# Graph kernel on one core: building the adjacency blocks with shorter loop bodies on TensorE and VectorE, and W stored from three pair buffers

## The chip, the cores and the metric

One core of a Trainium2 chip runs the whole program. The metric is the device time of one execution in microseconds, lower is better. Times in the profile are counted from the start of the span.

## The reference, cut to what matters

The reference is a chain of four graph layers over N = 3125 nodes (96 features) and E = 103,125 edges sorted by target. Each layer normalizes `x`, applies a graph operator and adds the result to `x`:

```python
h = relu(layernorm(x)); x = x + propagate_10_steps(h)        # counts of edges, degree-scaled
h = relu(layernorm(x)); x = x + gated_edges(h, edge_attr)    # per-edge gates, summed by target
h = relu(layernorm(x)); x = x + two_gcn_layers(h)            # segment_sum(h[src], dst)
h = relu(layernorm(x)); x = x + two_weighted_gcn(h, edge_weight)   # segment_sum(w * h[src], dst)
```

Every `segment_sum(h[src], dst)` is a product with a matrix that depends on the edges alone. The kernel builds two such matrices once, at its start: C, which counts the edges from each source to each target, and W, which sums their weights. This case is about that building stage alone.

## The kernel before

**The stages.** `edge_ranges` makes tables of the edges (to about 50 us), `build_matrices` makes C and W (about 50 to 545 us), `propagate` follows (to about 1137 us), then `gated_edges` (to about 2190 us), and the two GCN stages end the program.

**How the building is tiled.** The 3125 target nodes are padded to NT = 25 node tiles of 128. A node tile has WPT = 16 windows of WIN = 8 nodes, and GW = 4 windows make a group, so there are 400 windows and NG = 100 groups. For a group VectorE makes one-hot operands in one of two buffers: `S` (`sources` on L492, then `weighted` twice on L504, with the weight in two fp16 parts) and `M` (`targets` on L498). GpSimd makes the small columns that `targets` reads (L415, L421), and the column tile `sw` comes in by a DMA for each group (L444). For each window TensorE multiplies three edge tiles in three parts, which is 9 matmuls of 200 columns into one PSUM bank (`products`, L573). Where the table's flag `past` is over 0, there is a fourth edge tile and each of the four windows has 12 matmuls. Code for still more edges (`past > 1`: `one_more` on VectorE, `more_products` on TensorE) is in the loops, but is not executed on these inputs. ScalarE takes each window out of PSUM in two copies, L641 (counts, into the C block) and L645 (weights, into `Wwin`), and SyncE stores W window by window (L459) and C once for a node tile (L461). For `propagate` the C block of the tile before is also transposed, 25 transposes a tile after the second window of each group (`turn`, L592), and copied to `CT` (L632).

**The loops.** VectorE's loop (`four`, L546) has four groups in its body, 25 rounds. Each group's body holds `one_more` four times, once for each window. TensorE does the first node tile in straight code, and its loop (`four`, L619) then has four node tiles in its body, 6 rounds, so that it goes back to its start five times. ScalarE's and SyncE's loops have two node tiles each.

**What orders the work.** Semaphores alone. VectorE may start group g when TensorE has finished group g - 2 (`dve.wait_ge(s_built, g * GW + GW)`, on a counter that starts at 8). TensorE starts group g when VectorE has finished it (`s_made`), and a window when ScalarE has taken out the window four before it (`s_evac`). ScalarE may write a buffer of `Wwin` when the store of the window four before it has landed (`s_wst`); SyncE's queue serves its `sw` loads and its stores in the order of the code.

Of the kernel before, what the change touches and what calls it, by code (L numbers as in the profile page):

```python
# [13 lines left out]
ALU = mybir.AluOpType  # L14
# [19 lines left out]
FRONT = 2 * (GW - 1)  # L34
SWB = 4
SE = 6
NS = 135
# [286 lines left out]

def build_matrices(nc, tab_d, pair_d, key, smod, weight, CT, indeg, spare, C_d, W_d):

# [5 lines left out]
    with ExitStack() as ctx:  # L332
        m = Scope(nc, ctx, "build")
        tab = m.sb("tab", [1, NG + 1, GW + 2], I16)
        colsM = m.sb("colsM", [P, HALF, 2], F16)
# [18 lines left out]
        Sx = m.sb("Sx", [P, PARTS, P], F16)  # L354
        rowh = Cblk[0][:, 0, :]
        win = m.ps("win", [P, 4, 512])
# [16 lines left out]
        s_cst = [m.sem(f"C_stored{b}") for b in range(2)]  # L373
        s_wst = [m.sem(f"W_stored{r}") for r in range(4)]
        block = ctx.enter_context(nc.Block())

        def group_range(eng, regs, g):

            eng.load(regs, tab[0:1, bass.ds(g, 1), :])
            why = "edge_ranges clamps the tables"  # L380
            first = nc.s_assert_within(eng.snap(regs[0]), 0, FRONT + TCLAMP, skip_runtime_bounds_check_because=why)
            ends = [nc.s_assert_within(eng.snap(regs[1 + i]), 1, FRONT + TCLAMP + 1,
                                       skip_runtime_bounds_check_because=why) for i in range(GW)]
            return first, ends

        def group_over(eng, reg, g):
# [5 lines left out]
        def _(pool):  # L392
# [35 lines left out]
            with pool.Fori(0, NG // 2) as pair:  # L428
                columns(0, pair * 2)
                columns(1, pair * 2 + 1)  # L430
            columns(0, NG)

        @block.sync
        def _(sp):
            sp.dma_start(tab[:, :, :], tab_d[0:NG + 1, :].rearrange("(o q) b -> o q b", o=1)).then_inc(s_tab, 16)

            reg = sp.alloc_register("sp_bound")

            def columns(b, g):

                sp.load([reg], tab[0:1, bass.ds(g, 1), 0:1])
                t = nc.s_assert_within(sp.snap(reg), 0, FRONT + TCLAMP,
                                       skip_runtime_bounds_check_because="edge_ranges clamps the tables")
                sp.dma_start(sw[:, b, :, :, :].rearrange("p a t z -> p a (t z)"),  # L444
                             pair_d[:, :, bass.ds(t * 2, 2 * GT)]).then_inc(s_sw[b], 16)

            def store(j, b):

                for u in range(WPT):
                    if u % GW == 0:  # L450
                        g = j * (WPT // GW) + u // GW
# [9 lines left out]
                sp.dma_start(C_d[bass.ds(j, 1), :, :].rearrange("o p c -> p (o c)"),  # L461
                             Cblk[b].rearrange("p k d -> p (k d)")).then_inc(s_cst[b], 16)
# [10 lines left out]
            for r in range(4):  # L473
                sp.wait_ge(s_wst[r], 16 * (NW // 4) + 1)

        @block.vector
        def _(dve):
# [4 lines left out]
            dve.wait_ge(s_tab, 16)  # L482
            regs = [dve.alloc_register(f"dve_bound{r}") for r in range(GW + 2)]
            over = dve.alloc_register("dve_over")
# [10 lines left out]
            def targets(b):  # L495

                shape = [P, CH * GW, HALF, 2]
                nc.vector.tensor_tensor(M[:, b, :, :, :, :].rearrange("p c i a z -> p (c i) a z"),  # L498
                                        colsM[:, :, :].unsqueeze(1).to_broadcast(shape),
                                        kw[:, b, :, :, :].rearrange("p c i z -> p (c i) z").unsqueeze(2).to_broadcast(shape),  # L500
                                        ALU.is_equal)
# [5 lines left out]
            def one_more(b, i, t):  # L507

                dve.wait_ge(s_xused, dve.snap(more) + 1)
                n = dve.snap(more) * 6  # L510
                dve.reg_add(more, more, 1)
                nc.vector.tensor_tensor(kx[:, :], key[:, bass.ds(t, 1)], bases[:, b, i:i + 1], ALU.subtract).then_inc(s_xstep, 1)
                nc.vector.tensor_copy(wx[:, 0:1], weight[:, bass.ds(t, 1)]).then_inc(s_xstep, 1)
# [12 lines left out]
            def group(b, r, g, turn):  # L526
# [24 lines left out]
        def _(pe):  # L551
# [6 lines left out]
            for b in range(2):  # L558
                pe.sem_inc(s_cst[b], 1)
            for r in range(4):  # L560
                pe.sem_inc(s_wst[r], 1)
# [7 lines left out]
            def products(b, i, tiles):  # L569
                for u in tiles:  # L570
                    for part in range(PARTS):
                        out = win[:, i, 0:WC] if part == 0 else win[:, i, WC:2 * WC]
                        mm = pe.matmul(out, S[:, b, part, 2 * i + u, :, :].rearrange("p a z -> p (a z)"),  # L573
                                       M[:, b, u, i, :, :].rearrange("p a z -> p (a z)"),
                                       start=(u == 0 and part == 0), stop=(u == FEW - 1 and part in (0, PARTS - 1)),
# [9 lines left out]
            def turn(j, b, g):  # L585
# [9 lines left out]
            def node_tile(j, b, before):  # L595

                for q in range(WPT // GW):
# [3 lines left out]
                    for i in range(GW):  # L601
# [12 lines left out]
                        products(q % 2, i, range(FEW - 1, FEW)).then_inc(s_built, 1)  # L614
                        if before and i == 1:
                            turn(j - 1, 1 - b, q)
# [9 lines left out]
        def _(act):  # L626
# [9 lines left out]
            def node_tile(j, b, before):  # L636

                act.wait_ge(s_cst[b], (j - b) * 8 + 1)
                for u in range(WPT):
                    act.wait_ge(s_built, j * WPT + u + 1 + 2 * GW)  # L640
                    nc.scalar.activation(Cblk[b][:, :, u * WIN:(u + 1) * WIN],  # L641
                                         win[:, u % 4, 0:WC].rearrange("p (d k) -> p k d", d=WIN),
                                         ACT.Copy, scale=0.5).then_inc(s_evac, 1)
# [1579 lines left out]
def gnn(nc, x, src_cols, dst_cols, dst_rows, attr, w_cols, We, be, Wn, bn, W1, b1, W2, b2,  # L2223
# [10 lines left out]
    with ExitStack() as outer:  # L2234
# [5 lines left out]
        with ExitStack() as inner:  # L2240
# [3 lines left out]
            with ExitStack() as ctx:  # L2244
# [4 lines left out]
                edge_ranges(nc, src_cols, dst_cols, dst_rows, w_cols, tab_d, tabs_d, base_d, row_d, pair_d, key, smod, weight, unscale, CT)  # L2249
                build_matrices(nc, tab_d, pair_d, key, smod, weight, CT, indeg, xs, C_d, W_d)  # L2250
            propagate(nc, x, xs, CT, indeg, src_cols, We, be, Wn, bn, ident, first, P_d, Q_d)
# [45 lines left out]
```

## Time and profile before

| | us |
|---|---|
| median of three runs | 2706.46 |
| lowest and highest of them | 2706.18, 2714.7 |
| the profiled execution, its own time | 2699.71 |
| its span, first to last instruction | 2697.9 |
| building stage in it | about 50 to 545 |

The profiled execution gives durations and waits; its time is 6.75 us below the median of the three runs. A row that groups instructions has their count, their busy time, the mean of one, and the idle time of the engine just before them with what ended it. `PEld` is TensorE's weight load, and an engine name with a `q` is its sequencer (branches and register work).

### The profile page before, as it was taken

What the parts mean: (1) busy time and instruction counts of PE and PEld (TensorE: products, weight loads), DVE (VectorE), ACT (ScalarE), POOL (GpSimd) and SP (SyncE); (2) the same over time, 40 slices, a digit from 0 to 9 for tenths busy, and PEclk for the clock granted to TensorE, in tenths of its full rate; (3) what the DMA queues carried; (4) which work ended last, traced back from release to release, by engine and by line L of the source; (5) the groups of instructions that cost most, each with busy time, mean ns of one, the idle gap of its engine ahead of it and who ended that gap; (6) DMA issues with size and microseconds to landing.
All of it is one profiled execution on the core that took longest, in us unless ns stands there. A gap on an engine that the chain in (4) does not pass through costs nothing. (4 is left out here: it accounts for less than half of the span.)

```text
span 2697.9 us, 55857 instructions
## 1 busy us (share of the span) xinstructions
PE 2221.2 (82%) x18268; PEld 2088.8 (77%) x18269; DVE 1638.3 (61%) x3181; ACT 1356.5 (50%) x2800; POOL 1111.1 (41%) x1225
## 2 busy tenths in 40 slices
PE   2878788869999999687778877788788748779998
PEld 1877777869999999487677777777777648779998
DVE  7888778855433334566565666666666664465465
ACT  1666556643333332165555555555555523257686
POOL 2655556500000000277777777777777702200000
PEclk6999999989999999765555555555555569979999
DMA  1444444410000000444444444444444452096281
GB/s 58 143 131 128 133 128 141 135 45 2 2 2 1 2 2 16 118 118 116 108 113 113 109 117 108 111 115 109 117 109 110 109 213 104 2 385 226 79 292 39
DMA packets 184980, 283.92 MB, mean 105 GB/s; under 512 B 76675, under 2 KB 152678, under 8 KB 179270
## 3 DMA queue, kind: packets, MB, share of 16 engines
q1 hardware_dynamic: 145958, 200.50, 23.4%
q0 software_dynamic: 38688, 79.28, 11.5%
q8 instruction: 171, 2.80, 0.5%
q14 instruction: 163, 1.34, 0.2%
HBM read 210.52 MB, written 69.15 MB: 104 GB/s over the span
## 5 line engine op out<-in xcount | busy, mean ns | idle before, releaser
L1238 POOL DMA_INDIRECT layer_R<-source_terms,layer_srcs x800 | 781.7, 977 | 243.7 <-issue 243.7
L1470 PE MATMUL layer_zp<-layer_right,layer_left 96*128 96x192 f32 x1342 | 471.3, 536 | 178.9 <-DVE layer_left L1257 174.8
L1470 PEld LDWEIGHTS layer_zp<-layer_right,layer_left 96*128 96x128 f32 x1342 | 404.1, 327 | 195.7 <-DVE layer_left L1257 186.7
L1004 PEld LDWEIGHTS layer_acc<-layer_U,graph_CT 128*128 128x128 f16 x6250 | 524.7, 97 | 30.6 <-ACT layer_U L933 21.1
L1004 PE MATMUL layer_acc<-layer_U,graph_CT 128*128 128x192 f16 (+1 forms) x6250 | 529.8, 246 | 22.0 <-ACT layer_U L933 20.0
L573 PE MATMUL build_win<-build_M,build_S 128*128 128x200 f16 x3948 | 382.6, 253 | 127.3 <-DVE build_S L504 77.0
L573 PEld LDWEIGHTS build_win<-build_M,build_S 128*128 128x128 f16 x3948 | 335.3, 99 | 156.9 <-issue 45.6
L1491 PEld LDWEIGHTS layer_acc<-layer_hot,layer_G 128*98 128x98 f32 x1648 | 252.3, 256 | 114.9 <-DVE layer_aggT L1311 114.8
L1491 PE MATMUL layer_acc<-layer_hot,layer_G 128*98 128x32 f32 x1648 | 268.3, 329 | 54.0 <-DVE layer_aggT L1311 53.8
L2209 PE MATMUL layer_acc<-layer_V,layer_turn 128*128 128x96 f32 x2500 | 287.9, 278 | 0.6 <-issue 0.6
L2209 PEld LDWEIGHTS layer_acc<-layer_V,layer_turn 128*128 128x128 f32 x2500 | 286.0, 195 | 0.9 <-issue 0.9
L1416 ACT ACTIVATE layer_y<-layer_R 128x1152 f32<-128x1152 f32 x135 | 156.3, 1158 | 237.3 <-DVE layer_R L1285 237.3
L1285 DVE TENSOR_TENSOR layer_R<-layer_zp,layer_R 128x1152 f32<-128x1152 f32 x135 | 182.4, 1351 | 145.1 <-DMA layer_R<-source_terms,layer_srcs 144.9
L1227 POOL IOTA layer_place<- 128x1 f32 x1 | 0.1, 137 | 577.4 <-POOLq L680 577.4
L1290 DVE SCALAR_TENSOR_TENSOR layer_z<-layer_R,layer_y 128x576 f32<-128x576 f32 (+1 forms) x136 | 102.8, 756 | 213.4 <-ACT layer_y L1423 213.4
L415 POOL TENSOR_TENSOR build_bases<-build_bases,build_stride 128x4 f32<-128x4 f32 x101 | 156.6, 1550 | 181.7 <-DVE build_S L492 179.2
L2137 ACT ACTIVATE layer_turn<-layer_ring 128x2048 f32<-128x2048 f32 x49 | 200.9, 4114 | 30.1 <-PE layer_acc L2209 30.1
L1410 ACT ACTIVATE layer_gate<-layer_z 128x480 f32<-128x480 f32 x135 | 77.6, 574 | 220.7 <-DVE layer_z L1292 220.7
L2065 DVE COPY layer_turn<-layer_ring 128x1152 f32<-128x1152 f32 x49 | 116.8, 2385 | 110.5 <-PE layer_acc L2209 110.3
L824 DVE TENSOR_TENSOR layer_h<-layer_h,layer_acc 128x96 f32<-128x96 f32 x250 | 63.6, 254 | 196.9 <-ACT layer_h L951 193.8
L498 DVE TENSOR_TENSOR build_M<-build_colsM,build_kw 128x3200 f16<-128x3200 f16 x100 | 181.8, 1818 | 1.0 <-issue 0.6
L645 ACT ACTIVATE nodes_x<-build_win 128x200 f32<-128x200 f32 x400 | 137.0, 343 | 83.1 <-DMA W_blocks<-nodes_x 82.0
(312 smaller groups left out, 2890.4 us busy)
## 6 DMA issues: line engine op xcount, KB each, us to landing
layer_ring<-W_blocks SPq DMA_DIRECT2D x41, 1600.0 KB, 8.3
W_blocks<-nodes_x SPq DMA_DIRECT2D x400, 100.0 KB, 2.3
layer_left<-in_attr SPq DMA_DIRECT2D x68, 384.0 KB
layer_C<-C_blocks SPq DMA_DIRECT2D x25, 800.0 KB, 19.8
layer_R<-source_terms,layer_srcs POOLq DMA_INDIRECT x800
C_blocks<-nodes_x SPq DMA_DIRECT2D x13, 800.0 KB, 4.9
C_blocks<-build_Cblk SPq DMA_DIRECT2D x12, 800.0 KB, 4.8
layer_rows<-target_rows SPq DMA_DIRECT2D x68, 96.0 KB
```

The source lines that it names most:

```text
L415: nc.gpsimd.tensor_tensor(bases[:, b, :], bases[:, 1 - b, :], stride[:, :], ALU.add).then_inc(s_cols, 1)
L498: nc.vector.tensor_tensor(M[:, b, :, :, :, :].rearrange("p c i a z -> p (c i) a z"), colsM[:, :, :].unsqueeze(1).to_broadcast(shape), kw[: ...
L573: mm = pe.matmul(out, S[:, b, part, 2 * i + u, :, :].rearrange("p a z -> p (a z)"), M[:, b, u, i, :, :].rearrange("p a z -> p (a z)"), sta ...
L645: nc.scalar.activation(Wwin[:, u % 4, :], win[:, u % 4, WC:2 * WC], ACT.Copy).then_inc(s_evac, 1)
L1004: return pe.matmul(acc[:, k % RING, 0:columns], CT[:, t, k * P:(k + 1) * P], pairs[:, cur, t, 0:columns], start=(t == 0), stop=(t == NT - 1))
L1238: nc.gpsimd.indirect_dma_start(R[:, i, u, :], None, P_d, bass.IndirectOffsetOnAxis(ap=at_u, axis=0)).then_inc(s_R[i], 16)
L1285: nc.vector.tensor_tensor(R[:, i, 0:n, :], zp[h][:, 0:n, 0:D2], R[:, i, 0:n, :], ALU.add).then_inc(s_add, 1)
L1416: nc.scalar.activation(y[:, h, 0:n, :], R[:, i, 0:n, :], ACT.Abs).then_inc(s_abs, 1)
L1470: pe.matmul(out[u], left[:, i, u * P:(u + 1) * P], right[:, i, :], start=(u % 2 == 0), stop=False, skip_group_check=True)
L1491: mm = pe.matmul(acc[h][0:DG, 0:QW], G[:, h, u, :], hot[:, h, u, :], start=(u == 0), stop=(u == last))
L2137: nc.scalar.activation(turn[:, u % RT, 0:KA, :], ring[:, s, :, 0:KA].rearrange("p d k -> p k d"), ACT.Copy).then_inc(s_turn, 1)
L2209: mm = pe.matmul(acc[:, n % 4, 0:D], turn[:, (base + n) % RT, k, :], V[:, i, k, :], start=(k == 0), stop=(k == NT - 1))
```

## The change

The reading of edges, the arithmetic and the results stay as they are. The change does these things in `build_matrices`:

- TensorE's loop body is one node tile in place of four: an outer loop of 12 rounds holds an inner loop of 2. The C block that is transposed is then picked by a register (`Cblk[:, bass.ds(b, 1), k, :]`), and tile numbers are sums over two loop registers.
- VectorE's body still has four groups, but `one_more` stands once for each group, in a loop over the windows.
- W is stored for two windows at a time (200 KB in place of 100 KB, 200 stores in place of 400). There are three buffers of two windows, taken in the order 0, 1, 2, 0, 1, 2, 0, 1 within each node tile.
- Buffers move: `sw` into the space of a later `ident`, the table into a free part of `CT`, one half of `M` into `x`'s space, both C blocks side by side into a tile of their own. GpSimd leaves out its last call of `columns`.

```diff
+WSLOT = (0, 1, 2, 0, 1, 2, 0, 1)
...
-        tab = m.sb("tab", [1, NG + 1, GW + 2], I16)
+        TAB = (NG + 1) * (GW + 2)
+        tab = CT[0:1, NT - 1, 3 * ETK:3 * ETK + TAB].bitcast(I16).rearrange("p (q b) -> p q b", b=GW + 2)
...
-        sw = m.sb("sw", [P, SWB, PARTS, GT, 2], F16)
+        sw = later[:, 0:SWB * PARTS * GT].bitcast(F16).rearrange("p (r a t z) -> p r a t z", r=SWB, a=PARTS, z=2)
...
-        Wwin = words[:, CW:CW + 4 * WC].rearrange("p (r c) -> p r c", r=4)
-        M = m.sb("M", [P, 2, CH, GW, HALF, 2], F16)
+        Wtwo = [words[:, CW + 2 * WC * r:CW + 2 * WC * (r + 1)] for r in range(2)] + [m.sb("Wtwo", [P, 2 * WC], F32)[:, :]]
+        M = [words[:, 0:CW].bitcast(F16).rearrange("p (c i a z) -> p c i a z", c=CH, i=GW, z=2),
+             m.sb("M", [P, CH, GW, HALF, 2], F16)]
...
-        Cblk = [words[:, 0:CW].bitcast(F16).rearrange("p (k d) -> p k d", d=P), m.sb("Cblk", [P, NT, P], F16)]
+        Cblk = m.sb("Cblk", [P, 2, NT, P], F16)
...
-            columns(0, NG)
-
...
-                    sp.wait_ge(s_evac, j * (2 * WPT) + 2 * u + 2 + EVAC0)
-                    sp.dma_start(W_d[bass.ds(j, 1), :, u * WC:(u + 1) * WC].rearrange("o p c -> p (o c)"),
-                                 Wwin[:, u % 4, :]).then_inc(s_wst[u % 4], 16)
+                    if u % 2 == 1:
+                        sp.wait_ge(s_evac, j * (2 * WPT) + 2 * u + 2 + EVAC0)
+                        sp.dma_start(W_d[bass.ds(j, 1), :, (u - 1) * WC:(u + 1) * WC].rearrange("o p c -> p (o c)"),
+                                     Wtwo[WSLOT[u // 2]]).then_inc(s_wst[WSLOT[u // 2]], 16)
...
                 with dve.If(past > 1):
-                    first, ends = group_range(dve, regs, g)
-                    for i in range(GW):
-                        with dve.If(ends[i] > first + (2 * i + CH)):
-                            with dve.Fori(first + (2 * i + CH), ends[i], 1) as t:
+                    with dve.Fori(0, GW) as i:
+                        first, end = window_range(dve, regs, g, i)
+                        with dve.If(end > first + i * 2 + CH):
+                            with dve.Fori(first + i * 2 + CH, end, 1) as t:
                                 one_more(b, i, t)
...
                 for k in range(first, end):
-                    mm = pe.transpose(tp[:, g, k - first, :], Cblk[b][:, k, :], ident[:, :])
+                    mm = pe.transpose(tp[:, g, k - first, :],
+                                      Cblk[:, b, k, :] if isinstance(b, int) else
+                                      Cblk[:, bass.ds(b, 1), k, :].rearrange("p o d -> p (o d)"), ident[:, :])
...
-            node_tile(0, 0, False)
-            with pe.Fori(0, NT // 4) as four:
-                for u in range(4):
-                    node_tile(four * 4 + 1 + u, (1 + u) % 2, True)
+            node_tile(0, None, 0)
+            with pe.Fori(0, NT // 2) as pair:
+                with pe.Fori(0, 2) as old:
+                    node_tile(pair * 2 + old + 1, pair * 2 + old, old)
...
-                    act.wait_ge(s_wst[u % 4], j * 64 + u // 4 * 16 + 1)
-                    nc.scalar.activation(Wwin[:, u % 4, :], win[:, u % 4, WC:2 * WC], ACT.Copy).then_inc(s_evac, 1)
+                    r, done = WSLOT[u // 2], WSLOT[:u // 2].count(WSLOT[u // 2])
+                    if u % 2 == 0:
+                        act.wait_ge(s_wst[r], j * (16 * WSLOT.count(r)) + 16 * done + 1)
+                    nc.scalar.activation(Wtwo[r][:, u % 2 * WC:(u % 2 + 1) * WC], win[:, u % 4, WC:2 * WC], ACT.Copy).then_inc(s_evac, 1)
```

## Rows read from the trace of the kernel before

**Rows 1.** Groups by line, building stage (count, busy us, mean ns, idle before).

```profile
L573 PE MATMUL build_win<-build_M,build_S 128*128 128x200 f16 x3948 | 382.6, 253 | 127.3 <-DVE build_S L504 77.0 <-issue 32.6 <-ACT build_Cblk L641 8.0
```

**Rows 2.** Waits in the building stage (us in total, times, longest).

```profile
ACT nodes_x L645 <- DMA W_blocks<-nodes_x: 82.0, 101, 3.6
...
DVE build_S L492 <- PE build_win L573: 68.6, 36, 8.3
...
PEld build_win L573 <- ACT nodes_x L645: 41.0, 41, 3.2
...
PE build_win L573 <- ACT nodes_x L645: 6.8, 6, 3.0
```

**Rows 3.** Line L498, building stage (ns min/median/max, first and last start us).

```profile
L498 DVE TENSOR_TENSOR build_M<-build_colsM,build_kw x100: 1810/1818/1839, 55.0 to 536.1; 128x3200 f16<-128x3200 f16 x100
```

**Rows 4.** Timeline of VectorE, 197 to 219 us (start, us, idle before).

```profile
201.14 1.81 DVE L498 TENSOR_TENSOR build_M<-build_colsM,build_kw 128x3200 f16<-128x3200 f16 x1
...
205.74 0.83 DVE L492 TENSOR_TENSOR build_S<-build_colsS,build_sw 128x1280 f16<-128x1280 f16 x1 [1.30 <-PE build_win L573]
206.48 1.82 DVE L498 TENSOR_TENSOR build_M<-build_colsM,build_kw 128x3200 f16<-128x3200 f16 x1
...
210.46 1.81 DVE L498 TENSOR_TENSOR build_M<-build_colsM,build_kw 128x3200 f16<-128x3200 f16 x1
...
214.62 1.82 DVE L498 TENSOR_TENSOR build_M<-build_colsM,build_kw 128x3200 f16<-128x3200 f16 x1
```

**Rows 5.** Timeline of VectorE at the first and the last return of its loop.

```profile
72.35 0.82 DVE L492 TENSOR_TENSOR build_S<-build_colsS,build_sw 128x1280 f16<-128x1280 f16 x1 [1.17 <-issue]
...
523.02 0.82 DVE L492 TENSOR_TENSOR build_S<-build_colsS,build_sw 128x1280 f16<-128x1280 f16 x1 [1.12 <-issue]
```

**Rows 6.** Line L546, VectorE's sequencer at one return, 201 to 206 us.

```profile
L546 DVEq COMPARE_BRANCH  x1: 56/56/56, 201.9 to 201.9; - x1
L546 DVEq FUSED_REGOPS  x1: 80/80/80, 205.4 to 205.4; - x1
```

**Rows 7.** Line L1371, the same in the loop of `gated_edges`, 1199 to 1226 us.

```profile
L1371 DVEq COMPARE_BRANCH  x1: 56/56/56, 1221.5 to 1221.5; - x1
L1371 DVEq FUSED_REGOPS  x1: 198/198/198, 1221.8 to 1221.8; - x1
```

**Rows 8.** Timeline of VectorE at the first and last return of TensorE's loop.

```profile
160.20 0.83 DVE L492 TENSOR_TENSOR build_S<-build_colsS,build_sw 128x1280 f16<-128x1280 f16 x1 [7.51 <-PE build_win L573]
...
477.45 0.82 DVE L492 TENSOR_TENSOR build_S<-build_colsS,build_sw 128x1280 f16<-128x1280 f16 x1 [7.77 <-PE build_win L573]
```

**Rows 9.** Lines L619 (building) and L1509 (`gated_edges`): TensorE's loop branches.

```profile
L619 PEldq COMPARE_BRANCH  x6: 76/3906/4057, 146.8 to 542.5; - x6
...
L1509 PEldq FUSED_REGOPS  x33: 167/168/172, 1137.8 to 2105.5; - x33
...
L1509 PEldq COMPARE_BRANCH  x33: 76/208/217, 1164.0 to 2135.8; - x33
```

**Rows 10.** DMA queues, 226 to 305 us: one round of TensorE's loop.

```profile
q8 instruction: 14, 0.23, 1.3%
q14 instruction: 20, 0.16, 0.8%
```

**Rows 11.** DMA queues, 1200 to 2100 us: all that moved (packets, MB, share).

```profile
q0 software_dynamic: 33688, 69.04, 30.0%
q1 hardware_dynamic: 13216, 31.91, 14.6%
q14 instruction: 6, 0.05, 0.0%
```

**Rows 12.** Windows, 312 to 318 us (busy by engine, then PEclk, DMA, GB/s).

```profile
312.00:318.00 6.00, 5.65 (x41) 5.26 (x42) 0.00 (x0) 1.50 (x6) 0.00 (x0) 0.56 0.55 188
```

**Rows 13.** Timeline, 354 to 369 us, around a group with the fourth edge tile.

```profile
355.84 0.83 DVE L492 TENSOR_TENSOR build_S<-build_colsS,build_sw 128x1280 f16<-128x1280 f16 x1 [1.00 <-PE build_win L573]
...
357.50 0.41 PEld L592 LDWEIGHTS build_tp<-build_ident,nodes_x 128*128 128x128 f16 x6
```

**Rows 14.** Lines L603 and L632, 226 to 305 us: register work on two sequencers.

```profile
L603 PEldq FUSED_REGOPS  x64: 46/46/51, 230.4 to 304.1; - x64
...
L632 ACTq FUSED_REGOPS  x16: 64/66/69, 226.7 to 302.8; - x16
```

**Rows 15.** DMA issues by line (count, KB each, us to landing).

```profile
W_blocks<-nodes_x SPq DMA_DIRECT2D x400, 100.0 KB, 2.3
...
C_blocks<-nodes_x SPq DMA_DIRECT2D x13, 800.0 KB, 4.9
```

More of the change, by code:

```diff
@@ L322, in _, with build_matrices @@
                                         add, None, ALU.add).then_inc(s_tables, 1)
-def build_matrices(nc, tab_d, pair_d, key, smod, weight, CT, indeg, spare, C_d, W_d):
+def build_matrices(nc, tab_d, pair_d, key, smod, weight, CT, indeg, spare, later, C_d, W_d):
     NCOL = 3
@@ L354, in build_matrices @@
         Sx = m.sb("Sx", [P, PARTS, P], F16)
-        rowh = Cblk[0][:, 0, :]
+        rowh = Cblk[:, 0, 0, :]
         win = m.ps("win", [P, 4, 512])
@@ L373, in build_matrices @@
         s_cst = [m.sem(f"C_stored{b}") for b in range(2)]
-        s_wst = [m.sem(f"W_stored{r}") for r in range(4)]
+        s_wst = [m.sem(f"W_stored{r}") for r in range(3)]
         block = ctx.enter_context(nc.Block())
@@ L384, in group_range, with window_range @@
             return first, ends
+        def window_range(eng, regs, g, i):
+            why = "edge_ranges clamps the tables"
+            eng.load([regs[0]], tab[0:1, bass.ds(g, 1), 0:1])
+            eng.load([regs[1]], tab[0:1, bass.ds(g, 1), bass.ds(i + 1, 1)])
+            first = nc.s_assert_within(eng.snap(regs[0]), 0, FRONT + TCLAMP, skip_runtime_bounds_check_because=why)
+            end = nc.s_assert_within(eng.snap(regs[1]), 1, FRONT + TCLAMP + 1, skip_runtime_bounds_check_because=why)
+            return first, end
         def group_over(eng, reg, g):
@@ L472, in _ @@
                 sp.wait_ge(s_cst[b], 16 * (NT // 2 + 1 - b) + 1)
-            for r in range(4):
-                sp.wait_ge(s_wst[r], 16 * (NW // 4) + 1)
+            for r in range(3):
+                sp.wait_ge(s_wst[r], 16 * NT * WSLOT.count(r) + 1)
         @block.vector
@@ L482, in _ @@
             dve.wait_ge(s_tab, 16)
-            regs = [dve.alloc_register(f"dve_bound{r}") for r in range(GW + 2)]
+            regs = [dve.alloc_register(f"dve_bound{r}") for r in range(2)]
             over = dve.alloc_register("dve_over")
@@ L497, in targets @@
                 shape = [P, CH * GW, HALF, 2]
-                nc.vector.tensor_tensor(M[:, b, :, :, :, :].rearrange("p c i a z -> p (c i) a z"),
+                nc.vector.tensor_tensor(M[b][:, :, :, :, :].rearrange("p c i a z -> p (c i) a z"),
                                         colsM[:, :, :].unsqueeze(1).to_broadcast(shape),
@@ L507, in one_more @@
             def one_more(b, i, t):
+                base = bases[:, b, bass.ds(i, 1)]
                 dve.wait_ge(s_xused, dve.snap(more) + 1)
@@ L511, in one_more @@
                 dve.reg_add(more, more, 1)
[L512 removed]
+                nc.vector.tensor_tensor(kx[:, :], key[:, bass.ds(t, 1)], base, ALU.subtract).then_inc(s_xstep, 1)
                 nc.vector.tensor_copy(wx[:, 0:1], weight[:, bass.ds(t, 1)]).then_inc(s_xstep, 1)
@@ L559, in _ @@
                 pe.sem_inc(s_cst[b], 1)
-            for r in range(4):
+            for r in range(3):
                 pe.sem_inc(s_wst[r], 1)
@@ L591, in turn, with node_tile @@
                 for k in range(first, end):
-                    mm = pe.transpose(tp[:, g, k - first, :], Cblk[b][:, k, :], ident[:, :])
+                    mm = pe.transpose(tp[:, g, k - first, :],
+                                      Cblk[:, b, k, :] if isinstance(b, int) else
+                                      Cblk[:, bass.ds(b, 1), k, :].rearrange("p o d -> p (o d)"), ident[:, :])
                 mm.then_inc(s_tp, 1)
-            def node_tile(j, b, before):
+            def node_tile(j, before, old):
                 for q in range(WPT // GW):
@@ L614, in node_tile @@
                         products(q % 2, i, range(FEW - 1, FEW)).then_inc(s_built, 1)
-                        if before and i == 1:
-                            turn(j - 1, 1 - b, q)
-            node_tile(0, 0, False)
-            with pe.Fori(0, NT // 4) as four:
-                for u in range(4):
-                    node_tile(four * 4 + 1 + u, (1 + u) % 2, True)
+                        if before is not None and i == 1:
+                            turn(before, old, q)
+            node_tile(0, None, 0)
+            with pe.Fori(0, NT // 2) as pair:
+                with pe.Fori(0, 2) as old:
+                    node_tile(pair * 2 + old + 1, pair * 2 + old, old)
             for g in range(len(TG)):
@@ L2249, in gnn @@
                 edge_ranges(nc, src_cols, dst_cols, dst_rows, w_cols, tab_d, tabs_d, base_d, row_d, pair_d, key, smod, weight, unscale, CT)
-                build_matrices(nc, tab_d, pair_d, key, smod, weight, CT, indeg, xs, C_d, W_d)
+                build_matrices(nc, tab_d, pair_d, key, smod, weight, CT, indeg, xs, ident, C_d, W_d)
             propagate(nc, x, xs, CT, indeg, src_cols, We, be, Wn, bn, ident, first, P_d, Q_d)
```

6 lines of the change are left out of this document (3 added, 3 removed).

## The prediction

> **What bounds the kernel now.** I first looked at the groups by line for the building stage, since the diff touches nothing else, and at the waits there. VectorE and TensorE hold each other: TensorE's matmuls stand idle mostly for VectorE's operands [rows 1], and VectorE stands idle for TensorE 68.6 us in 36 waits [rows 2]. So I read the pace of the stage from one instruction that VectorE does once in each group, L498. Its 100 starts run from 55.0 to 536.1 us [rows 3], which is 481.1 us for 99 periods, 4.86 us each. The timeline shows what such a period is when nothing stops it: 206.48 to 210.46, 3.98 us, all of it VectorE's own four instructions back to back. The next is 4.16 (210.46 to 214.62), and the one before is 5.34 (201.14 to 206.48) [rows 4]. At 3.98 us throughout, the stage would take 99 x 3.98 = 394.0 us. So 87.1 us are stops, and the question is whose.
>
> **Stop 1, VectorE's loop returns, 24 of them.** The long period of [rows 4] ends at the return of VectorE's loop. Its sequencer reads the loop branch at 201.9 and the first register instruction of the next round only at 205.4 us, 3.5 us later [rows 6]. In the loop of gated_edges the same two stand 0.3 us apart [rows 7]. Meanwhile the instructions already queued run out, and the engine is idle 1.1 to 1.3 us: 1.17 at the first return, 1.12 at the last [rows 5], 1.30 in between [rows 4]. The name behind the arrow differs, the sequencer's gap doesn't. Against 3.98 the period is 1.36 longer; I take 1.3: 24 x 1.3 = 31 us.
>
> **Stop 2, TensorE's loop returns, 5 of them.** TensorE's loop branch takes 3906 ns at the median in the building stage and 208 ns in gated_edges [rows 9]. VectorE then waits 7.51 us at the first such return and 7.77 at the last, five alike [rows 8], with 8.3 the longest [rows 2]. After a return the granted clock is down as well, 0.56 in one such stretch [rows 12], near the lower of its two levels (1.2 and 2.4 GHz), after TensorE had stood still; so it catches up at about half speed. I take 7.5: 5 x 7.5 = 37.5 us.
>
> **What both are.** While TensorE goes once round its loop, the queue that brings it instructions moves 14 packets and 0.23 MB, 16 KB each, and the other instruction queue 20, which is 5 for each of the four rounds that VectorE makes in that time [rows 10]. In 900 us of gated_edges, some 27 rounds of its loops, TensorE's queue doesn't appear at all and the other has 6 packets [rows 11]. So a short loop stays with its engine, and a long one is brought again in every round.
>
> **Stop 3, groups with a fourth edge tile.** 3948 matmuls less 400 x 9 are 348, or 29 groups with 12 more [rows 1]. Such a group makes VectorE wait 1.00 us [rows 13]. The rest of the 87.1, 87.1 - 31 - 37.5 = 18.6 us, holds those of the 29 that show now and small steps such as the 0.18 of [rows 4]. The other ones hide under stops 1 and 2, since TensorE catches up while VectorE stands at its loop return.
>
> **The change, part by part.**
>
> *VectorE's body.* The one_more code stands 4 times in place of 16, and it is most of the instructions of the body. 5 packets a round were the whole body; with three quarters of its largest part gone, it should be 2 to 3. I price stop 1 at nothing afterwards: -31 us. The added inner loop and window_range are never executed here. The small step of 0.18 at a group's start, likely a jump over the same code, goes too.
>
> *TensorE's body.* 14 packets for four tiles are 3.5 for one. The branch then costs what L1509's does: -37.5 us. The clock dip goes with it.
>
> *What comes back.* With stops 1 and 2 gone, all 29 long groups show, 29 x 1.0 = 29 us. The stage is then 394.0 + 29 = 423.
>
> *TensorE's new register work.* The nearest row for an operand placed by a register is ScalarE's L632, one FUSED_REGOPS of 66 ns for each instruction; TensorE's own measure 46 [rows 14]. Each of 24 x 25 = 600 transposes needs one: between nothing (each stands beside a weight load; six of them take 0.41 us, about 70 ns each [rows 13]) and 600 x 66 = 40 us. Waits with two loop registers add a little to the 46 ns of L603. I take 4 us, near the hidden end, because a transpose and its register step are of about equal length. The returns are 24 to 35 in place of 5, at 168 + 208 ns [rows 9] each: 24 x 0.38 = 9 us if bare, nothing if TensorE waits for VectorE there anyway. I take half, 4 us. Nothing else is queued behind them on TensorE but the next group, for which VectorE waits.
>
> *W in pairs.* ScalarE waits 82.0 us for W's stores, 101 times [rows 2], but TensorE's matmuls wait for that copy only 6.8 us, its weight loads 41.0 [rows 2], and much of it ends in time that TensorE waits anyway. With three pairs, a pair is filled again six windows later in place of four. Only across a tile's end is it tighter: pair 6 ends in slot 0 and the next tile starts in slot 0, three windows on. A store of 200 KB lands between 2.3 us (100 KB) and 4.9 (800 KB) [rows 15]; by line between the two about 2.7. Three windows are 3 of the 4 in a 3.98 us period, so about 3.0 us: a wait of 0 to 0.5 there, twice a tile. Bounds: -7 (all of the 6.8 gone) to +0.5 x 2 x 24 = +24, if every one reached VectorE. SyncE issues 200 fewer DMAs, and its loads of sw come no later. I take 0.
>
> *Moved buffers, GpSimd's last call.* Same sizes and engines; the last call lies behind VectorE's last group, and nothing waits for it but the end of the stage. 0, with TensorE still transposing meanwhile.
>
> **The sum.** 423 + 4 + 4 = 431 us against 481.1: -50 us. The profiled execution's 2699.7 becomes 2649.7. It lies 6.75 us below the median of the runs, so by the median 2706.5 - 50 = 2656.5 us.
>
> **A rule of the Trainium skill, weighed.** The page "Runtime: NRT & Kernel Launch", section "Instruction fetch mechanics", says that an engine holds a small window of instructions (for TensorE 128 KiB, for the others 32 KiB), and that a taken branch out of it makes a fetch that is waited for. By that rule the trace agrees: 14 packets of 16 KB are 224 KB and refetched, 3.5 of them are 56 KB and would stay, and VectorE's 5 packets of 8 KB are 40 KB, over 32. The page "Advanced Engine Details and Errata", section "ISA Cache", adds that there are only two lines, of 256 instructions each. Read strictly for TensorE that speaks against this change, for one tile's body would be out of the window as well; rival B is what it would do.
>
> **The rivals.**
>
> *A, TensorE becomes the pace.* The period of an ordinary group has little room: VectorE may start the group after next only when TensorE is done. If the register steps of the transposes and of the waits are bare, 40 us [rows 14] in place of my 4, and the returns 9, the stage is 423 + 49 = 472 and the time about 2697; half of it, the likelier form, gives about 2680. For it: TensorE's sequencer also has two branches in each window. Against: the matmuls go on from TensorE's queue while the sequencer works.
>
> *B, the short body isn't kept.* TensorE's loop of gated_edges, which is kept, may be much shorter than 3.5 packets; the rows show no length between it and 14. If each of 24 returns is a fetch, stop 2 is 24 x 7.5 = 180 in place of 37.5, and with stop 1 gone and some of the long groups hidden again the time is 2706 + 142 - 31 - 0 to 4, about 2815. It decides the sign from some seven more returns than now on, for 50 / 7.5 = 6.7. So a fetch at the outer loop's 11 returns alone would already use up most of the gain.
>
> *C, VectorE's body isn't short enough.* Stop 1 stays, fewer long groups show: -37.5 + 8, about 2677. Likewise if the new kernel's loop returns are quick but something else waits there.
>
> *D, W's stores wait at each tile's end.* +12 to +24 on the sum: about 2672.
>
> **How the numbers follow.** Forecast 0.66 (its own range 2646 to 2667), A 0.12, B 0.07, C 0.06, D 0.09. The lower end takes every bound in favour: 423 alone and W's -7 make -65, 2641. The upper end reaches over D and C and the half form of A, to 2690. Left out are B, the full form of A and little else. By 0.3% (8 us, about what a measurement of this kernel can tell): faster 0.89, within 0.04, slower 0.07.
>
> **What would show it.** The starts of L498 lie about 4.3 us apart in the mean, 427 to 436 in all, with no period over 6. The loop branch of TensorE takes about 0.2 us; its instruction queue has few packets between 120 and 540 us (14 in each round now, [rows 10]), and the other one under 10 in 79 us. VectorE's waits for TensorE are then nearly all of about 1 us, some 29. PEclk stays at 1.00 through the stage. Wrong would be: branches of 3 to 4 us at every tile (B), L492 waiting in most groups by 0.1 to 0.5 us (A), returns of VectorE still 3.5 us long (C), L645 waiting at a tile's first and third window, with TensorE waiting for it (D).

## The result, and the profile after

The changed kernel takes 2670.45 us (median of four runs, 2668.4 to 2671.28), the kernel before beside it 2710.12 us (2706.18 to 2714.7): ratio 0.9852, 95% interval 0.9831 to 0.9873. That is 39.7 us less; against the 2706.46 us that the prediction started from it is 36.0. The forecast was 50, to 2656.5. In a later set of runs it took 2673.87 us against 2708.95, ratio 0.9862 (0.9827 to 0.9898).

Profiled execution to profiled execution the gain is smaller, 2699.7 to 2671.3 us, or 28.4, since the one of before lies at the low end of what that kernel does (its runs here go from 2693.6 to 2716.5 us). All but 1 us of the 28.4 is in the building stage. The starts of the `targets` instruction, now L509 and under two names because M's buffers lie apart:

```profile
L509 DVE TENSOR_TENSOR nodes_x<-build_colsM,build_kw x50: 1810/1819/1827, 54.9 to 504.1; 128x3200 f16<-128x3200 f16 x50
L509 DVE TENSOR_TENSOR build_M<-build_colsM,build_kw x50: 1811/1819/1826, 58.9 to 508.7; 128x3200 f16<-128x3200 f16 x50
```

From 54.9 to 508.7 us are 453.7 (from the unrounded starts), against 481.1 [rows 3] and the 431 of the forecast. I call this number the stage time below. Outside it the two profiled executions differ by 1 us; over all kernels below the rest of the span goes from 2211.6 to 2218.6 us, which is why the stage time is the finer measure.

Both long stops are gone. The page's instruction queues, whose packets were 171 and 163 before:

```profile
q8 instruction: 93, 1.52, 0.2%
q14 instruction: 41, 0.34, 0.0%
```

Between 120 and 480 us neither queue moves a packet. TensorE's two loop branches, the outer (L634) and the inner (L635), against the 3906 ns of [rows 9]:

```profile
L634 PEldq COMPARE_BRANCH  x12: 67/208/209, 112.4 to 516.0; - x12
...
L635 PEldq FUSED_REGOPS  x24: 163/168/177, 75.4 to 497.8; - x24
...
L635 PEldq COMPARE_BRANCH  x24: 76/142/208, 94.2 to 515.8; - x24
```

And VectorE's return (L559), the branch and the next register instruction 0.3 us apart, where [rows 6] had 3.5:

```profile
L559 DVEq COMPARE_BRANCH  x1: 56/56/56, 215.3 to 215.3; - x1
L559 DVEq FUSED_REGOPS  x1: 80/80/80, 215.6 to 215.6; - x1
```

The granted clock is 1.00 from 100 to 500 us, as forecast. But the waits of the stage (us in total, times, longest) show what holds it now, where [rows 2] had 68.6 us in 36 waits, over half of that time at the five returns:

```profile
ACT build_Cblk L656 <- PE build_win L586: 173.0, 272, 10.4
...
PE build_win L586 <- DVE build_S L515: 52.4, 23, 43.1
DVE build_S L503 <- PE build_win L586: 50.1, 65, 2.2
PEld build_win L586 <- DVE build_S L515: 45.5, 3, 43.2
PEld build_win L586 <- ACT nodes_x L662: 36.2, 43, 1.8
...
PE build_win L586 <- ACT nodes_x L662: 19.3, 14, 1.6
```

VectorE waits for TensorE 65 times and never over 2.2 us; the forecast had some 29 waits of 1 us. TensorE's matmuls hardly wait for VectorE any more: of the 52.4 us, 43.1 are the one wait before the first window, which leaves 9.3 us. The same wait stands in the row of before, where 77.0 less 43.0 are 34.0 us:

```profile
PE build_win L573 <- DVE build_S L504: 77.0, 51, 43.0
```

ScalarE's copy L662 no longer waits for a store at all, as its groups by line show (the last number is its idle time before):

```profile
L662 ACT ACTIVATE nodes_x<-build_win 128x200 f32<-128x200 f32 x300 | 101.7, 339 | 0.0
...
L662 ACT ACTIVATE build_Wtwo<-build_win 128x200 f32<-128x200 f32 x100 | 33.9, 339 | 0.0
```

TensorE's timeline over one node tile's end shows two places (start, us, idle before):

```profile
236.94 1.52 PEld L586 LDWEIGHTS build_win<-build_M,build_S 128*128 128x128 f16 x18 [0.84 <-ACT build_Wtwo L662]
238.44 0.68 PEld L605 LDWEIGHTS build_tp<-build_ident,build_Cblk 128*128 x6
239.15 1.53 PEld L586 LDWEIGHTS build_win<-build_M,build_S 128*128 128x128 f16 x18
242.12 2.00 PEld L586 LDWEIGHTS build_win<-nodes_x,build_S 128*128 128x128 f16 x24 [1.45 <-ACT nodes_x L662]
```

Six transposes take 0.68 us in place of 0.41 [rows 13], and at the tile's end the loads stand still for 1.45 us. The name behind that arrow misleads: in that gap TensorE's sequencer is busy with the inner loop's return, which begins at 240.7, and the next tile's first window step (L618) comes at 242.0. From the return's first step to the tile's first weight load it is 1.4 to 1.9 us at each of the loop's tiles but the first, whatever ScalarE does. Line L635 at that return, L605 (its register steps, one ahead of each transpose) in the six transposes, and L618:

```profile
L635 PEldq ALU_OP  x1: 36/36/36, 240.7 to 240.7; - x1
L635 PEldq COMPARE_BRANCH  x1: 208/208/208, 240.8 to 240.8; - x1
L635 PEldq FUSED_REGOPS  x1: 168/168/168, 241.1 to 241.1; - x1
...
L605 PEldq FUSED_REGOPS  x6: 46/46/46, 238.3 to 238.9; - x6
...
L618 PEldq FUSED_REGOPS  x2: 46/46/46, 242.0 to 242.6; - x2
```

Six register steps start within 0.6 us, one each 0.12 us, though each is shown with 46 ns. They are bare only where the sequencer isn't ahead of the engine: another six transposes, from 248.1, take 0.41 us as in the kernel before. VectorE's wait comes one group later, 1.83 us:

```profile
246.96 0.82 DVE L503 TENSOR_TENSOR build_S<-build_colsS,nodes_ident 128x1280 f16<-128x1280 f16 x1 [1.83 <-PE build_win L586]
```

That place repeats. Of the 50 us that VectorE waits for TensorE, 29 stand at one group of the four in a tile, the one that may start when TensorE has finished the tile's first group.

So after the result my theory was number 1 below: the missing 20 us are TensorE's own register work, sized at 8 in the prediction. The rivals were ScalarE's copies, which stand behind many of the arrows, and for the other direction a two-tile body that would not be kept.

### The profile page after: what moved, and what is told of

The parts are those of the page before. It is cut to its first block and busy times, and to the rows that moved or that the text cites. A ratio compares the mean times of both kernels' runs of the same rounds, so it can differ in the third digit from the quotient of the medians.

```text
span 2669.5 us, 55867 instructions
## 1 busy us (share of the span) xinstructions
PE 2247.4 (84%) x18268; PEld 2104.9 (79%) x18269; DVE 1639.3 (61%) x3181; ACT 1355.3 (51%) x2800; POOL 1112.4 (42%) x1222
## 5 line engine op out<-in xcount | busy, mean ns | idle before, releaser
L1487 PE MATMUL layer_zp<-layer_right,layer_left 96*128 96x192 f32 x1342 | 477.0, 541 | 170.5 <-DVE layer_left L1274 167.9
L1487 PEld LDWEIGHTS layer_zp<-layer_right,layer_left 96*128 96x128 f32 x1342 | 409.6, 330 | 186.8 <-DVE layer_left L1274 179.4
L1508 PEld LDWEIGHTS layer_acc<-layer_hot,layer_G 128*98 128x98 f32 x1648 | 260.8, 263 | 108.9 <-DVE layer_aggT L1328 108.5
L1508 PE MATMUL layer_acc<-layer_hot,layer_G 128*98 128x32 f32 x1648 | 275.7, 334 | 48.0 <-DVE layer_aggT L1328 47.9
L586 PE MATMUL build_win<-nodes_x,build_S 128*128 128x200 f16 x1944 | 188.5, 252 | 73.7 <-DVE build_S L515 46.2
L586 PEld LDWEIGHTS build_win<-nodes_x,build_S 128*128 128x128 f16 x1944 | 160.3, 99 | 91.3 <-DVE build_S L515 44.6
L656 ACT ACTIVATE build_Cblk<-build_win 128x200 f16<-128x200 f32 x400 | 135.9, 340 | 174.1 <-PE build_win L586 173.0
L586 PE MATMUL build_win<-build_M,build_S 128*128 128x200 f16 x2004 | 191.2, 250 | 13.1 <-DVE build_S L515 6.2
L586 PEld LDWEIGHTS build_win<-build_M,build_S 128*128 128x128 f16 x2004 | 165.0, 98 | 28.0 <-ACT build_Wtwo L662 9.8
```

The source lines that it names most:

```text
L656: nc.scalar.activation(Cblk[:, b, :, u * WIN:(u + 1) * WIN], win[:, u % 4, 0:WC].rearrange("p (d k) -> p k d", d=WIN), ACT.Copy, scale=0.5 ...
L1487: pe.matmul(out[u], left[:, i, u * P:(u + 1) * P], right[:, i, :], start=(u % 2 == 0), stop=False, skip_group_check=True)
L1508: mm = pe.matmul(acc[h][0:DG, 0:QW], G[:, h, u, :], hot[:, h, u, :], start=(u == 0), stop=(u == last))
```

## The experiments

All kernels are the changed kernel with the edit shown; stage times are those of their profiled executions, and medians and ratios are against runs of the kernel before on the same chip.

**Two tiles in TensorE's body, written out.**

```diff
             with pe.Fori(0, NT // 2) as pair:
-                with pe.Fori(0, 2) as old:
-                    node_tile(pair * 2 + old + 1, pair * 2 + old, old)
+                node_tile(pair * 2 + 1, pair * 2, 0)
+                node_tile(pair * 2 + 2, pair * 2 + 1, 1)
```

> The changed kernel with two node tiles in TensorE's loop body, written out, so that the C block is picked by a constant and the loop has one level. Measure: first to last start of L509 (one-hot targets), 453.7 us in the changed kernel. Theory 1 (TensorE's sequencer: 600 register steps for the transposes and 24 costlier returns cost the missing 22 us): 425 to 438 us, the time 16 to 28 us under the changed kernel's. Theory 2 (ScalarE's copies hold TensorE, not its own code): within 3 us of 453.7. Theory 3 (a body of some seven 16 KB packets is not kept): 11 branches of 3 to 4 us, 500 us or more.

2638.65 us against 2700.3, ratio 0.9773 (0.9755 to 0.9791). The stage time is 424.8 us, 28.9 under the changed kernel's; by the two ratios, which come from different sets of runs, it is some 21 us. Theory 1 stands, theories 2 and 3 fall. The starts, the branch, and the waits:

```profile
L509 DVE TENSOR_TENSOR nodes_x<-build_colsM,build_kw x50: 1810/1818/1826, 54.5 to 475.3; 128x3200 f16<-128x3200 f16 x50
L509 DVE TENSOR_TENSOR build_M<-build_colsM,build_kw x50: 1809/1818/1827, 58.5 to 479.3; 128x3200 f16<-128x3200 f16 x50
...
L634 PEldq COMPARE_BRANCH  x12: 76/208/212, 108.8 to 485.4; - x12
```

```profile
DVE build_S L503 <- PE build_win L586: 25.0, 31, 1.3
```

31 waits with 25.0 us, none over 1.3: these are the long groups of stop 3, forecast as 29 at 1.00. The prediction's sum without register work was 394.0 + 29 = 423 us; here are 424.8. At the group that waits for a tile's first one VectorE now waits 7.0 us in all, where the changed kernel has 29. A body of two tiles (seven packets by the count of [rows 10]) stays with TensorE just as one does: no packet of its queue between 120 and 480 us. The six transposes take 0.41 us again:

```profile
217.89 0.41 PEld L605 LDWEIGHTS build_tp<-build_ident,build_Cblk 128*128 128x128 f16 x6
```

**The same body, with the C block picked by a register.**

```diff
             with pe.Fori(0, NT // 2) as pair:
-                node_tile(pair * 2 + 1, pair * 2, 0)
-                node_tile(pair * 2 + 2, pair * 2 + 1, 1)
+                pe.reg_mov(which, 0)
+                node_tile(pair * 2 + 1, pair * 2, picked())
+                pe.reg_mov(which, 1)
+                node_tile(pair * 2 + 2, pair * 2 + 1, picked())
```

`picked()` reads the register `which`, declared to be 0 or 1.

> The same two-tile body, but the C block is picked by a register that is set to 0 or 1 ahead of each tile: 600 register steps as in the changed kernel, with returns as in the two-tile kernel. Theory 1, if the register steps are the larger part: 8 to 18 us slower than the two-tile kernel; if the returns are: under 5 us slower. Theory 2: no difference.

2656.68 us, ratio 0.9838 (0.9816 to 0.9859), on the same chip as the kernel above and 18.0 us slower. The stage time is 444.5, so picking the block by a register costs 19.7 us, somewhat over the 8 to 18 that I expected. The register steps are there again, with the same length:

```profile
L605 PEldq FUSED_REGOPS  x111: 46/46/51, 226.0 to 302.3; - x111
```

The 19.7 us hold a little more than these 600 steps: at each tile's start two steps for the pick (the `reg_mov` and `picked()`) stand ahead of the table's load. At the group that waits for a tile's first one VectorE waits 21.1 us in all here, between the 7.0 and the 29. What is left to the changed kernel's 453.7, 9.2 us, goes with 24 inner and 12 outer loop branches in place of 12 plain ones, and tile numbers from two registers. I have not separated these.

**One test in place of two in ordinary windows**, on top of the two-tile body.

```diff
                         with pe.If(past > 0):
                             products(q % 2, i, range(FEW, CH))
-                        with pe.If(past > 1):
+                            with pe.If(past > 1):
                                 first, ends = group_range(pe, regs, g)
```

> The two-tile kernel with TensorE's test past > 1 inside the test past > 0, so that an ordinary window has one branch in place of two (400 windows, 284 of them ordinary, 0.2 us each). Theory 1 (the sequencer still lags the array in ordinary groups): 2 to 10 us faster than the two-tile kernel. If VectorE's 3.98 us sets the pace of those groups once the register steps are gone: within 2 us.

2636.7 us against the two-tile kernel's 2638.65 on the same chip, stage time 423.6 against 424.8. That is within 2 us by both, as the second expectation has it. With VectorE at 3.98 us a group and the long groups to pay for, little more is in TensorE's sequencer. It is the fastest of the study: ratio 0.9767 (0.9748 to 0.9785).

**W window by window, in the changed kernel.** The four buffers and the 400 stores of before.

```diff
-                    if u % 2 == 1:
-                        sp.wait_ge(s_evac, j * (2 * WPT) + 2 * u + 2 + EVAC0)
-                        sp.dma_start(... (u - 1) * WC:(u + 1) * WC ..., Wtwo[WSLOT[u // 2]]) ...
+                    sp.wait_ge(s_evac, j * (2 * WPT) + 2 * u + 2 + EVAC0)
+                    sp.dma_start(... u * WC:(u + 1) * WC ..., Wwin[:, u % 4, :]) ...
```

> The changed kernel with W stored window by window from four buffers as before. My prediction gave the pairs 0 us: then within 3 us of the changed kernel. If the 82 us of ScalarE's waits for W's stores reached VectorE now that the other stops are gone: 5 to 15 us slower, with waits of TensorE for L662's place longer than the 19.3 us of the changed kernel.

2666.16 us, ratio 0.9876 (0.9855 to 0.9897), which overlaps the changed kernel's; stage time 451.2 against 453.7 and, in its second run, 453.4. So the pairs are worth nothing in this kernel, as forecast; if anything it is 2 us the other way.

**W window by window, in the fastest kernel.** The same edit on the two-tile kernel with the nested test.

> The two-tile kernel with the nested test, and W stored window by window. If the pairs are worth nothing, as in the changed kernel (451.2 against 453.7 us without them): 421 to 426 us against 423.6, the time within 3 us. If the stores' waits come to the front once nothing else holds TensorE: 427 to 435 us, with L662's place waiting for DMAs and TensorE waiting for it.

Stage time 429.4 against 423.6, so 5.8 us more, inside the second expectation. Ratio 0.9762 (0.9727 to 0.9796), which can't tell it from 0.9767: it ran on another set of runs, with 6 us more outside the stage. The waits:

```profile
ACT nodes_x L660 <- DMA W_blocks<-nodes_x: 70.9, 72, 3.4
...
PEld build_win L586 <- ACT nodes_x L660: 46.0, 59, 1.7
...
DVE build_S L503 <- PE build_win L586: 26.8, 30, 2.3
```

The stores' waits are there, and TensorE's loads wait longer for the copy, 46.0 us, where the kernel with pairs has 20.9 and 6.4 (two names) and next to no wait for a store (0.2 us). But little of it reaches VectorE, whose waits for TensorE are 26.8 us against 25.0. A larger part of the 5.8 us stands right before `targets`, 3.3 us in nine places against 0.2 in one. There VectorE's sequencer loads the group's flag from the table, which takes 289 ns at the median and here up to 893:

```profile
204.27 1.83 DVE L509 TENSOR_TENSOR nodes_x<-build_colsM,build_kw 128x3200 f16<-128x3200 f16 x1 [0.45 <-issue]
...
L401 DVEq TENSOR_LOAD <-graph_CT x100: 283/289/893, 54.1 to 483.7; - x100
```

Why those loads are slow is not shown. The changed kernel with the same stores has none over 539 ns on VectorE, so the stores alone don't bring them. What the pairs are worth in this kernel stays between some 2 us and 5.8, from one execution each.

**TensorE's old body of four tiles, written out.**

```diff
-            with pe.Fori(0, NT // 2) as pair:
-                with pe.Fori(0, 2) as old:
-                    node_tile(pair * 2 + old + 1, pair * 2 + old, old)
+            with pe.Fori(0, NT // 4) as four:
+                for u in range(4):
+                    node_tile(four * 4 + 1 + u, four * 4 + u, u % 2)
```

> The changed kernel with TensorE's old body of four node tiles, written out (C block by a constant), and all else as changed. The two-tile kernel took 18 us less than the same with register picks. Here the five long returns are back: branches of about 3.9 us. My prediction priced the returns at 37.5 us together: 25 to 38 us slower than the two-tile kernel, so within some 15 us of the changed kernel, on either side. If TensorE's long returns cost less now that VectorE's own are gone: under 20 us.

2684.92 us, ratio 0.9916 (0.989 to 0.9942), stage time 468.1: 43.3 over the two-tile kernel, 14.4 over the changed one. The five long returns are back, with their branch and VectorE's waits of up to 10.5 us:

```profile
L634 PEldq COMPARE_BRANCH  x6: 76/3364/3618, 142.6 to 528.6; - x6
...
DVE build_S L503 <- PE build_win L586: 67.3, 36, 10.5
```

43.3 us for five is 8.7 each, somewhat over the 25 to 38 that I expected, priced at 7.5. A return holds two stops and not one. After the branch the first weight load goes, and then the loads stand again:

```profile
224.61 0.10 PEld L586 LDWEIGHTS build_win<-nodes_x,build_S 128*128 128x128 f16 x1 [3.63 <-issue]
227.67 2.77 PEld L586 LDWEIGHTS build_win<-nodes_x,build_S 128*128 128x128 f16 x17 [2.96 <-issue]
```

All five returns look like this, with 2.3 to 3.7 us for the second stop. From 228 to 233 us the granted clock is then 0.50, the lower level, while TensorE works without a pause.

**VectorE's old body, in the changed kernel.** (`one_more` four times in each group, TensorE's one-tile body kept.)

```diff
-                    with dve.Fori(0, GW) as i:
-                        first, end = window_range(dve, regs, g, i)
-                        with dve.If(end > first + i * 2 + CH):
-                            with dve.Fori(first + i * 2 + CH, end, 1) as t:
+                    first, ends = group_range(dve, regs, g)
+                    for i in range(GW):
+                        with dve.If(ends[i] > first + (2 * i + CH)):
+                            with dve.Fori(first + (2 * i + CH), ends[i], 1) as t:
                                 one_more(b, i, t)
```

> The changed kernel with the code for more edges four times in each group of VectorE's body, as before. My prediction: 24 returns at 1.3 us, less long groups hidden under them again. In the changed kernel TensorE holds the pace, so that VectorE's returns may lie under its lag: 5 to 20 us slower than the changed kernel. At or under 3 us, VectorE's short body was worth nothing while TensorE's is register-bound.

2682.51 us, ratio 0.9901 (0.9867 to 0.9935), stage time 466.3: 12.6 over the changed kernel. As expected, VectorE's returns lie partly under TensorE's lag.

**VectorE's old body with the two-tile body.**

> The two-tile kernel with VectorE's long body. Measure: first to last start of L509, 424.8 us in the two-tile kernel, 468.1 with TensorE's four-tile body, 496.1 with both bodies long, 466.3 with TensorE's one-tile body and VectorE's long one. If the two stops add up: 424.8 + (496.1 - 468.1) = 453 us. If VectorE's returns hide the long groups as my prediction says, they cost less here than 24 x 1.3 = 31: 443 to 450 us. If they cost more, as in the kernel with the one-tile body (12.6 more than the changed kernel, under a TensorE that lags), there is another coupling.

2673.82 us, ratio 0.9867 (0.9831 to 0.9903), stage time 460.6: 35.8 over the two-tile kernel, where I had expected 28 if the stops add up and less if they hide. One of its returns:

```profile
201.43 0.82 DVE L503 TENSOR_TENSOR build_S<-build_colsS,nodes_ident 128x1280 f16<-128x1280 f16 x1 [1.63 <-PE build_win L586]
202.39 1.83 DVE L509 TENSOR_TENSOR nodes_x<-build_colsM,build_kw 128x3200 f16<-128x3200 f16 x1
```

Its L509 starts at 202.39, the one before at 196.50, so that period is 5.89 us, 1.9 over 3.98; in the mean over the 24 returns it is 5.62 in place of the 4.28 that the two-tile kernel has there. That is 32.2 of the 35.8 us; the other 3.6 are spread over the other periods, and what couples them is open.

**Pairs and moved buffers alone**, both loop bodies as long as before.

> W in pairs and the moved buffers alone: both loop bodies as long as before. My prediction: the same as the kernel before, within 4 us. If the stores' waits on ScalarE mattered: 4 to 12 us faster than before, and no wait of L662 for a DMA.

2713.05 us against 2706.23, ratio 1.0019 (1.0002 to 1.0035). No gain; if anything 0.19%, some 5 us, is lost, where I had expected less than 4 us either way. The stage time of its profiled execution, 496.1, is 15 over the 481.1 of before, but those two executions don't lie alike: 2714.65 is near its median of 2713, and 2699.7 is low for a kernel with medians of 2706 to 2710. Outside the stage the two have the same 2216.8 us, so the 15 us between these executions are all in the stage. Why the kernel may be slower is open.

**The changed kernel again.**

> The changed kernel as it is, timed beside the next two. Within 5 us of its 2670.45 us, and L509's starts again some 450 to 456 us apart from first to last.

2673.87 us, stage time 453.4.

The four combinations of loop bodies, pairs everywhere, stage time in us:

| TensorE's body | VectorE's long | VectorE's short |
|---|---|---|
| four tiles | 496.1 | 468.1 |
| two tiles, written out | 460.6 | 424.8 |
| one tile, by register (the change) | 466.3 | 453.7 |

## Why the prediction was right in its direction and short in its size

*The bound and the floor* were right. 3.98 us for a group, 99 times, and a further 1.0 us for each of 29 long groups gave 423 us; with no register work in the way the stage took 424.8. That the two agree so closely is partly luck: the waits are 25.0 us and not 29, and 5.8 us are small steps in the other periods, whose middle value is 4.03 and not 3.98. One reading was wrong without harm: TensorE's idle time "mostly for VectorE's operands" was 77.0 us, but 43.0 of it come before the first window, and the 34.0 that are left are about as much as the 32.6 of `issue` beside them [rows 1].

*Stop 2*, TensorE's returns: right in mechanism, a little small. Five cost 43.3 us once VectorE's are gone, against 37.5 priced from VectorE's idle time alone. Such a return is a branch of 3.4 us, a second stop of 2.3 to 3.7, and a first group at the lower clock. Why it costs VectorE more here than in the kernel before is not shown.

*Stop 1*, VectorE's returns: right in mechanism, too small too. Between the two-tile kernels they cost 35.8 us, between the four-tile kernels 28.0; I took 31 and let 10.4 come back as long groups that no longer hide. The sum of stops 1 to 3 (down 58) compares with 481.1 - 424.8 = 56.3 from profile to profile, and with 61.6 by the medians of the two-tile kernel.

*What failed is the term for TensorE's new register work.* I took 4 us for the register steps of the transposes, "near the hidden end, because a transpose and its register step are of about equal length", and 4 for the returns. Measured are 19.7 and 9.2, and 431 - 8 + 28.9 = 452 is the stage of 453.7. The shown length of a register step, 46 ns, is not what it takes from the sequencer: the steps follow each other at 0.12 us, against 0.07 for a transpose alone [rows 13], so the two are not of equal length. Nor is all of it bare: 600 times the 0.05 us between them would be 30 us, an estimate from these rows. It shows where the sequencer has no lead. In the changed kernel an ordinary group of TensorE takes 3.7 us from its first weight load to its last, under VectorE's 3.98, but the first group of a tile takes 3.96 and stands 1.19 us before it in the mean (3.4, 3.5 and 0.55 in the two-tile kernel). So one group in four is over VectorE's pace, and 23 of the 28.9 us lie in the period of VectorE that waits for it, 5.28 us in place of 4.35. The prediction had said that nothing but the next group is queued behind a return; that next group is what VectorE waited for.

*Rival A* had the right mechanism, with VectorE waiting in 65 of the groups as its sign has it, and was given 0.12. Its half form was also miscounted: 423 + 24.5 = 447.5 us is a time of 2673 us and not 2680, which is some 6 us from the measured stage and 3 from the time. (Rival C's 2677 leaves out the 8 us of register work in the same way; with them it is 2685.) The waits that A expected at 0.1 to 0.5 us are 0.8 in the mean, and three periods are over 6 us, where the forecast had none.

*Luck in the time.* The forecast fell 10 to 14 us short by the medians, but its stage was off by 22.7: the stage lost 27.4 us and not 50. The two differ because the stops were read from one execution at the low end, while the time was reckoned from the median. By the rest of the span, 2216.8 us, an execution at that median has a stage of some 488 us (an estimate), so that the old kernel had about 7 us more of stops than the 87.1 that the prediction divided. That error and the too small register term partly cancel in the time.

*Returns at a tile's end* cost more than a branch and a register instruction, 0.38 us. In the timeline above, 1.3 us pass from the return's first step at 240.7 to the first window's step at 242.0, with the table's load in it.

*W in pairs at 0* was right for the changed kernel. The tight place that rival D named, a tile's end, never waits: L662's idle time is 0.0 us. In the study's fastest kernel the pairs may be worth 2 to 5.8 us.

*The rule on the held window* agreed, and its strict form fell: rival B gave 2815 us if a body of 3.5 packets were not kept. Neither it nor one of seven (twice 3.5, not counted) is fetched again. Two lines of 256 instructions, as the section "ISA Cache" of the Trainium skill's page "Advanced Engine Details and Errata" has it, is not what TensorE shows here; the 128 KiB that the Trainium skill's page "Runtime: NRT & Kernel Launch" gives in its section "Instruction fetch mechanics" lie between the seven packets kept and the fourteen fetched again.

## What to carry to other kernels

If a loop's branch takes microseconds and the instruction queue moves the same number of packets in each round, the body is too long; cut it until the packets stop, and no further. Two tiles written out beat one tile in two nested loops by 29 us of 454 here, 20 of them because the transposes' addresses are then constants and need no register step, the rest at the loop's ends. Bound such a step by the distance between two of them on a busy sequencer, not by the length that the row shows, and look for the group in which the sequencer has no lead, which here is the first after a loop's return: an engine with slack in most groups can still hold another up there.

## What the runs showed of the hardware

- The kernels with both long bodies scatter most. The kernel before ran from 2697.72 to 2716.49 us in the set of 14 runs, the one with pairs alone from 2707.37 to 2718.4 in ten; the two-tile kernel from 2637.55 to 2639.96 in five. With one long body it is less clear: 4.5 us in five runs and in four, 6.3 in four, while the fastest kernel with single stores, which has none, has 6.5 in four.
- A fetch that is waited for takes some 3.4 to 3.9 us at a return on TensorE (median of the branch, 3364 and 3906 ns), with a second stop behind it, and 3.5 on VectorE's sequencer, of which its queued instructions hide all but 1.1 to 1.6.
- How fast a store lands goes with the loop bodies more than with its size. 200 KB take 1.9 us in the changed kernel (2.4 with both bodies long), 100 KB take 1.7 in the changed kernel with single stores and 2.3 in the kernel before [rows 15], where I had put 2.7 for 200 KB. C's 800 KB take 3.4 us wherever TensorE's body is short, VectorE's long or not, and 4.0 to 4.9 with four tiles in it. That the instruction packets cause this is not shown; they go through the same DMA engines. The lines of the changed kernel's profile:

```profile
W_blocks<-nodes_x SPq DMA_DIRECT2D x150, 200.0 KB, 1.9
...
C_blocks<-build_Cblk SPq DMA_DIRECT2D x25, 800.0 KB, 3.4
```
